# Path flags of a time-warping alignment: from VectorE comparisons to GpSimd differences and ScalarE signs

## The reference, cut to what matters

```python
def _align_one(small, large):              # for each of 32 batch elements
    D = _pairwise_euclidean(small, large)  # 256 x 256 distances
    R = _dtw_cost(D)                       # R[i,j] = D[i,j] + min(R[i-1,j], R[i,j-1], R[i-1,j-1])
    i_idx, j_idx, valid = _backtrack(R, T_small, T_large)  # from the last corner: argmin of diag, up, left
    contrib = small[i_idx] * valid[:, None].astype(small.dtype)
    return jnp.zeros((T_large, d)).at[j_idx].add(contrib)
x = x + jnp.tanh(g_xattn[1]) * vmap(_align_one)(ctx_1024, _layernorm(x, axis=-1))
```

## Time and profile before

| what | value |
|---|---|
| median of three runs | 1813.73 us |
| profiled execution, first to last instruction (span) | 1810.7 us |
| DVE busy, whole span | 1489.1 us (82%) |
| PE / ACT / POOL busy, whole span | 1379.4 / 1135.9 / 644.9 us |
| steps of the alignment, 1133.16 to 1370.00 us | DVE busy nearly throughout |
| hops L1537, x255 | 120.7 us busy, 473 ns each |
| TensorE granted clock in the alignment | 0.50 |

### The profile page before, as it was taken

One profiled execution on the slowest core, in us unless ns is written; L12 is line 12 of the kernel. 1 busy time (PEld: TensorE's weight loads), 2 busy tenths in 40 slices (PEclk: granted clock), 3 DMA queues, 4 the chain that ended last, 5 costly groups with the idle time before them and its releaser, 6 DMA issues. The chain is left out here.

```text
span 1810.7 us, 37501 instructions
## 1 busy us (share of the span) xinstructions
PE 1379.4 (76%) x11461; PEld 1067.0 (59%) x11461; DVE 1489.1 (82%) x4194; ACT 1135.9 (63%) x2463; POOL 644.9 (36%) x1094
## 2 busy tenths in 40 slices
PE   4899999999999999999999984233332004899996
PEld 4577878888888888888888764000001003666664
DVE  7777877878878787788877753999998998999995
ACT  4567677776777767777677662243334002999997
POOL 3333343433434334343343322200000003787785
PEclk7999999999999999999999996555555556999999
DMA  6444544445444454444544311322220002223321
GB/s 173 137 128 115 149 123 118 137 122 154 123 117 139 120 154 123 118 141 122 152 125 120 99 36 28 96 60 61 60 42 8 0 0 84 74 89 98 96 77 48
DMA packets 322942, 179.56 MB, mean 99 GB/s; under 512 B 93793, under 2 KB 318193, under 8 KB 322802
## 3 DMA queue, kind: packets, MB, share of 16 engines
q1 hardware_dynamic: 322802, 178.07, 35.2%
HBM read 122.91 MB, written 50.33 MB: 96 GB/s over the span
## 5 line engine op out<-in xcount | busy, mean ns | idle before, releaser
L1031 DVE TENSOR_REDUCE nmax<-s 128x2 f32<-128x512 f32 x512 | 327.5, 681 | 7.6 <-PE s L465 6.6
L737 ACT ACTIVATE pts<-s 128x512 f32<-128x512 f32 x512 | 282.3, 617 | 75.0 <-PE s L482 74.8
L1143 POOL TENSOR_TENSOR r<-rl 128x512 f32<-128x512 f32 x128 | 133.4, 1042 | 260.8 <-ACT rl L767 217.9
L465 PE MATMUL s<-kst,qst 96*128 96x256 bf16 x1024 | 158.7, 276 | 10.9 <-DVE nmax L1031 6.9
L482 PE MATMUL s<-qst,kst 128*128 128x256 bf16 x1024 | 160.3, 276 | 8.7 <-ACT pts L737 7.2
L1421 PE MATMUL gate<-diag,one 128*128 128x512 f16 x35 | 21.2, 607 | 171.9 <-DVE left L1512 171.9
L767 ACT ACTIVATE rl<-wb,fscl 128x256 f32<-128x256 f32 x256 | 108.0, 477 | 64.8 <-PE wb L568 64.8
L564 PE MATMUL wb<-x2l,wfcT 128*128 128x256 f32 x512 | 143.3, 302 | 0.7 <-ACT dd L789 0.7
L1000 DVE TENSOR_TENSOR r2l<-r,r2h 128x512 fp32r<-128x512 f32 x128 | 88.6, 692 | 66.0 <-POOL r L1143 40.3
L496 PE MATMUL oacc<-pts,vw 128*32 128x256 f32 x2048 | 137.9, 387 | 5.3 <-ACT pts L737 5.2
L431 PE MATMUL wb<-wprT,r2l 128*128 128x256 f32 x512 | 130.5, 293 | 6.9 <-DVE r2l L1000 6.9
(11 more groups left out here) (304 smaller groups left out, 4630.9 us busy)
## 6 DMA issues: line engine op xcount, KB each, us to landing
kst<-k_parts_dram SPq DMA_DIRECT2D x384, 64.0 KB, 2.6
qst<-q_parts_dram SPq DMA_DIRECT2D x384, 64.0 KB, 2.4
k_parts_dram<-kp SPq DMA_DIRECT2D x32, 384.0 KB, 5.4
q_parts_dram<-qp SPq DMA_DIRECT2D x32, 384.0 KB, 3.1
xin<-in_x_dram SPq DMA_DIRECT2D x32, 256.0 KB, 2.8
cT_raw<-in_ctx_T_dram SPq DMA_DIRECT2D x32, 256.0 KB, 5.4
xres<-in_x_dram SPq DMA_DIRECT2D x32, 256.0 KB, 3.1
cin<-in_ctx_dram SPq DMA_DIRECT2D x32, 256.0 KB, 4.7
```

Source lines behind the costliest of these rows:

```text
L465: last = pe.matmul(s1[h % 2][:, t, :], qst[b.p][0:MAXROW, h, t * P:t * P + P], kst[b.p][0:MAXROW, h, :], start=True, stop=True)
L737: act.activation(pt[h % (2 * HPG)], s2[h % 2][:], ACT.Exp).then_inc(e["expd"], 1)
L1031: v.tensor_reduce(nmax[:, T * h:T * h + T], s1[h % 2][:], AX.X, ALU.max, negate=True)\
L1143: pool.tensor_tensor(r2[:], rl[:, k % 2], rl[:, k % 2], ALU.mult)\
```

## The change

VectorE no longer makes `diag` and `left`. GpSimd subtracts instead, after every half step of 4 rows (`compare`): up minus diagonal, and left minus `best`, both into `between` (128 x 2 x 4 x 64, float32). ScalarE turns them into signs in float16 (`sign`), and TensorE weighs the signs with 0.5 and -512 into `gate`, whose row now has a 65th element, column 0. Column 0 gets the carry from the neighbour block by two small matrix products (`shift16`, `edge16`), so `top`, `carry_on` and the tile `carry` go. The decision scan runs in two halves of 4x65 elements, each 10 rows behind the first row of its half (`BEHIND`), and `far` has three buffers. The exchange of R between blocks is also made in halves; it waits until GpSimd has read what it overwrites (`compared`), and `best` of a half waits for the same. GpSimd's tables for the last layer are spread over steps 3 to 8, and its splitting of `b1` comes after the last `compare`.

```diff
+HROWS = ROWS // 2
+BEHIND = ROWS + 2
...
+            def compare(s, h):
+
+                u, p = 2 * s + h, s % 2
+                pool.wait_ge(chained, u + 1)
+                if s >= 1:
+                    pool.wait_ge(exchanged, u - 1), pool.wait_ge(flags, u - 1)
+                up_diag, row_left = apart[h][:, 0], apart[h][:, 1]
+                if h == 0:
+                    before = cost[1 - p][:, ROWS - 1, :]
+                    pool.tensor_tensor(up_diag[:, 0, :], before[:, 1:BW + 1], before[:, 0:BW], ALU.subtract)
+                lo, hi = HROWS * h + (h == 0), HROWS * h + HROWS
+                above = cost[p][:, lo - 1:hi - 1, :]
+                pool.tensor_tensor(up_diag[:, lo - HROWS * h:, :], above[:, :, 1:BW + 1], above[:, :, 0:BW], ALU.subtract)
+                pool.tensor_tensor(row_left, cost[p][:, some(h), 0:BW], best[:, some(h), :], ALU.subtract)\
+                    .then_inc(compared, 1)
...
+            for s in range(NSTEP):
+                for h in range(2):
+                    compare(s, h)
+                last_layer_tables(s - 3)
             pool.wait_ge(b1_in, 16)
...
+            def exchange(s, h):
+
+                act.wait_ge(chained, 2 * s + h + 1), act.wait_ge(compared, 2 * s + h)
                 for k in range(NBLK - 1):
...
-            def carry_on(s):
...
+            def sign(s, h):
+
+                u = 2 * s + h
+                act.wait_ge(compared, u + 1)
+                if s >= 1:
+                    act.wait_ge(gated, u - 1)
+                act.activation(signs[h][:], apart[h][:], ACT.Sign, bias=smallest[:, 0:1]).then_inc(flags, 1)
...
+                if 1 <= s < NSTEP:
+                    exchange(s - 1, 1)
+                if 1 <= s <= NSTEP:
+                    sign(s - 1, 1)
                 if s + 1 < NSTEP:
                     root(s + 1)
                 if s >= 2:
                     evacuate(s - 2)
                 if s < NSTEP - 1:
-                    exchange(s)
-                if 1 <= s < NSTEP:
-                    carry_on(s - 1)
+                    exchange(s, 0)
+                if s < NSTEP:
+                    sign(s, 0)
...
+            def gates_of(s, h):
+                u, q = 2 * s + h, s % 3
+                if s >= 1:
+                    pe.wait_ge(lasted, u - 1)
+                if s >= 1:
+                    pe.matmul(gate[h][:, :, 0], shift16[:], far[q - 1][:, some(h), BW], start=True, stop=False)
+                pe.matmul(gate[h][:, :, 0], edge16[:], unit[:, some(h)], start=(s == 0), stop=True)
+                pe.wait_ge(flags, u + 1)
+                pe.matmul(gate[h][:, :, 1:BW + 1], half16[:], signs[h][:, 0], start=True, stop=False)
+                pe.matmul(gate[h][:, :, 1:BW + 1], left16[:], signs[h][:, 1], start=False, stop=True).then_inc(gated, 1)
...
+            def behind(r):
+
+                u, at = (r - BEHIND) // HROWS, (r - BEHIND) % HROWS
+                if u >= 0 and at == 0:
+                    last_up(u // 2, u % 2)
...
                     prev = cost[p][:, i - 1, :] if i else cost[1 - p][:, ROWS - 1, :]
+                    if first and s >= 1:
+                        v.wait_ge(compared, u - 1)
                     ch.tick(v.tensor_tensor(best[:, i, :], prev[:, 1:BW + 1], prev[:, 0:BW], ALU.min))
-                    v.tensor_tensor(diag[p][:, i, :], prev[:, 0:BW], prev[:, 1:BW + 1], ALU.is_le)
-                    if i == 0 and s >= 1:
-                        v.wait_ge(exchanged, s)
+                    if first and s >= 1:
+                        v.wait_ge(exchanged, u - 1)
                     ch.hold()
...
-                    if i:
-                        v.tensor_tensor(left[p][:, i - 1, :], best[:, i - 1, :], cost[p][:, i - 1, 0:BW], ALU.is_gt)
-                    if i == ROWS // 2 and s >= 1:
-                        top(s - 1)
...
+                    behind(r)
```

More of the change, by code:

```diff
@@ L54 @@
 LEFT = 1024.0
+HROWS = ROWS // 2
+BEHIND = ROWS + 2
+CENTRE = LEFT / 2 + 0.5
+SMALLEST = 2.0 ** -126
 class Batch:
@@ L1224, in alignment_phase @@
         best = sb("best", [P, ROWS, BW])
[L1225 to L1228, removed]
+        apart = [sb(f"between{u}", [P, 2, HROWS, BW]) for u in range(2)]
+        signs = [sb(f"signs{u}", [P, 2, HROWS, BW], F16) for u in range(2)]
+        far = [sb(f"far{p}", [P, ROWS, BW + 1], F16) for p in range(3)]
         step = [sb(f"step{p}", [P, ROWS, BW], F16) for p in range(2)]
-        adds = sb("adds", [P, ROWS, BW])
-        one16, neg16, left16 = o["one16"], sb("neg16", [P, P], F16), sb("left16", [P, P], F16)
+        adds, smallest = sb("adds", [P, HROWS, BW + 1]), sb("smallest", [P, 1])
+        unit = sb("unit", [P, ROWS], F16)
+        one16, neg16, half16, left16 = o["one16"], sb("neg16", [P, P], F16), sb("half16", [P, P], F16), sb("left16", [P, P], F16)
+        shift16, edge16 = sb("shift16", [P, P], F16), sb("edge16", [P, P], F16)
         steps = sb("steps", [NB, S, S], F16)
@@ L1234, in alignment_phase @@
         hop, path = sb("hop", [NB, S]), sb("path", [NB, S + 1])
-        gate = [ctx.enter_context(nc.psum_tensor(f"gate{p}", [P, ROWS, BW], F32)) for p in range(2)]
+        gate = [ctx.enter_context(nc.psum_tensor(f"gate{h}", [P, HROWS, BW + 1], F32)) for h in range(2)]
         diff = [ctx.enter_context(nc.psum_tensor(f"diff{p}", [P, ROWS, BW], F32)) for p in range(2)]
@@ L1251, in alignment_phase @@
         g_in = [sem(f"g_in{p}") for p in range(2)]
-        (consts, zeroed, rooted, chained, flags, exchanged, gated, topped, lasted, carried, diffed, stepped, rch, held,
+        (consts, zeroed, rooted, chained, compared, flags, exchanged, gated, lasted, carried, diffed, stepped, rch, held,
          turned, copied, pch) = (sem(n) for n in (
-            "consts2", "zeroed", "rooted", "chained", "flags", "exchanged", "gated", "topped", "lasted", "carried",
+            "consts2", "zeroed", "rooted", "chained", "compared", "flags", "exchanged", "gated", "lasted", "carried",
             "diffed", "stepped", "row_chain", "held", "turned2", "path_cp", "pool_chain2"))
@@ L1262, in quad, with some @@
             return slice(NB * k, NB * k + NB)
+        def some(h):
+            return slice(HROWS * h, HROWS * h + HROWS)
         def loaded(s):
@@ L1308, in _ @@
             pc = Chain(pool, pch)
-            for p in range(2):
-                pc.link(pool.memset(carry[p][:], -2.0))
+            pc.link(pool.memset(smallest[:], SMALLEST))
+            for tile, value, base in ((half16, 0.5, 0), (left16, -LEFT / 2, 0), (one16, 1.0, 0), (neg16, -1.0, 0),
+                                      (shift16, 1.0, NB)):
+                pc.link(pool.memset(tile[:], 0.0))
+                pc.link(pool.affine_select(out=tile[:], in_=tile[:], compare_op=ALU.not_equal, fill=value,
+                                           base=base, pattern=[[-1, P]], channel_multiplier=1))
@@ L1311, in _ @@
+            pc.link(pool.memset(edge16[:], 0.0))
+            pc.link(pool.affine_select(out=edge16[0:NB, :], in_=edge16[0:NB, :], compare_op=ALU.not_equal,
+                                       fill=-CENTRE - 2.0, base=0, pattern=[[-1, P]], channel_multiplier=1))
+            pc.link(pool.memset(unit[:], 1.0))
             pc.link(pool.memset(adds[:], 2.0))
             pc.link(pool.memset(adds[:, :, 0:1], 2 * LEFT))
[L1313 to L1316, removed]
@@ L1325, in _ @@
[L1325 to L1331, removed]
@@ new lines, in last_layer_tables @@
+            def last_layer_tables(k):
+                if k == 0:
+                    pc.link(pool.memset(ones[:], 1.0))
+                    pc.link(pool.memset(o["identb"][:], 0.0))
+                    pc.link(pool.affine_select(out=o["identb"][:], in_=o["identb"][:], compare_op=ALU.not_equal, fill=1.0,
+                                               base=0, pattern=[[-1, P]], channel_multiplier=1))
+                elif k == 1:
+                    pc.link(pool.iota(o["iota"][:], pattern=[[1, S]], base=0, channel_multiplier=0,
+                                      allow_small_or_imprecise_dtypes=True))
+                    pool.sem_inc(l_consts, 1)
+                elif k == 2:
+                    pc.link(pool.memset(o["w1T"][:, C, :], 0.0))
+                elif k == 3:
+                    pc.link(pool.memset(shift[:, 0:1], MAGIC + 1.0))
+                    pc.link(pool.memset(shift[:, 1:2], 2.0))
+                elif k == 4:
+                    pc.link(pool.iota(iota[:], pattern=[[1, S]], base=0, channel_multiplier=0,
+                                      allow_small_or_imprecise_dtypes=True))
+                elif k == 5:
+                    pc.link(pool.memset(ident[:], 0.0))
+                    pc.link(pool.affine_select(out=ident[:], in_=ident[:], compare_op=ALU.not_equal, fill=1.0,
+                                               base=0, pattern=[[-1, NB]], channel_multiplier=1))
+                    pool.sem_inc(consts, 1)
@@ L1351, in root @@
```

(52 more changed lines are left out.)

25 lines of the change are left out of this document (8 added, 17 removed).

## The result

The changed kernel takes 1832.83 us (median of four runs, 1831.24 to 1834.11) against 1812.99 us (four runs) for the kernel before: 1.0106 times as long, 95% interval 1.0087 to 1.0125. It is 19.8 us slower; 29 were forecast, a median of 1843 us in a range of 1802 to 1880. The profiled execution spans 1829.5 us, 18.8 more than before.

A forecast was written before the change was run, and what follows sets the result against it. VectorE was taken to set the time. A new step of 5.04 + 1.04 + 1.5 = 7.6 us, 34 times, less 231.2 plus 2.0, gave +29 us: 1843 us, range 1802 to 1880 for 8 in 10.

The forecast's parts named there:

- The row is a dependent chain, and the comparisons lie in its gaps: VectorE's rows: without `diag` and `left` a row takes 0.63 us, eight 5.04 instead of 5.28.
- The half scans cost 0.52 each: Decision scan on VectorE: 260 elements take 0.64 us, less 0.12 idle anyway; 0.52 each, 1.04 a step.
- GpSimd's reads block `best` and the row scans, once each: VectorE's two-SBUF-input instructions wait while GpSimd reads SBUF: 1.5 us a step lost, 0.40 per 256-element read.
- the 192 elements: GpSimd's 192-element read for a step's first half: forecast to cost VectorE 0.30 us.
- the read of 64: GpSimd's 64-element read for a step's first half: forecast to cost VectorE nothing.
- The relay is hidden: GpSimd, ScalarE and TensorE between a half's last row and its decision scan: costed at nothing, 1 to 3 us to spare.
- the rival of a late relay: Half scan or `best` waits for the relay: at 0.5 us a half, step 8.6 us, time 1877 us; chance 0.12.
- The small terms: Outside the steps: step 0 +0.5 us, tail +0.5, bias parts reaching into the hops +1.0; together 2.0.
- The slots set the row: VectorE's rows: row 0.52 us, port loss 0.9, step 6.1, time 1792 us; rival, chance 0.16.
- The port costs little: GpSimd reads as quickly as its squares, 0.9 us a step; step 6.74, 1814 us, no change; rival, chance 0.10.

The follow-up runs named there:

- the experiment that does not read: Changed kernel with GpSimd's subtractions replaced by fills with 1.0, which write SBUF and read nothing: 1792.58 us, ratio 0.989.

## Why the prediction was right, and what it mis-sized

- *The row is a dependent chain, and the comparisons lie in its gaps.* Right: 0.65 in the five kernels without them, 0.63 forecast. The semaphores of the first row of a half, with two waits, add 0.07 each; the forecast left them out.
- *The half scans cost 0.52 each.* They cost 0.46: 0.58 from start to next start (1202.82 to 1203.40), not 0.64. The element price of 0.0019, drawn through the row scan's 0.26, was too low and the base too high: between the two decision scans, 1.13 for 512 and 0.58 for 260, an element costs 0.0022. Rows, half scans and waits together make 6.19 a step in the experiment that does not read, against 6.08 forecast.
- *GpSimd's reads block `best` and the row scans, once each.* Right in kind: the long ones stand where GpSimd reads, they go when it only writes, and the half scan is free. Mis-sized: 1.5 us a step forecast, 1.1 measured (7.28 less 6.19). This is the step of the sum that failed. It took 0.40 for a read of 256 elements, on the ground that GpSimd gets in when VectorE's read ends and holds VectorE for 0.51 us from there, less 0.12. In the trace GpSimd's instruction is already 0.2 us old when VectorE's next request comes (1201.11 and 1201.33; 1204.68 and 1204.90): its recorded start lies inside the VectorE instruction before. VectorE is let go 0.54 us after GpSimd's start (0.58 by the earlier trace rows), and so loses a little over 0.3. The first read of the second half cost only 0.17. The first half's scan lost 0.31, as much as was put down for the 192 elements; but it starts 0.01 us before that read, while the read of 64, put at nothing, is still running (1200.36 to 1200.69), and no run parts the two. 34 steps of 0.4 are 14 us; the rows, half scans and waits, forecast too short, took 4 of them back, and 1843 became 1833. That the two misses have opposite signs is luck.
- *The relay is hidden.* Right: one wait of 2.1 us, in the tail; so the rival of a late relay fell too. ScalarE's work came to 3.9 us a step (131.52 in 34), 3.8 forecast; before it was 2.5 (82.40 in 33 steps), not 3.1, which changes nothing in the sum.
- *The small terms.* Step 0 took 5.7 instead of 5.3 us, the tail 7.56 instead of 7.40, the hops 0.7 more: 1.3 together against 2.0.
- *The other rivals.* "The slots set the row" fell with the kernel before without comparisons, and with the bare rows of 0.65. "The port costs little" had the loss to the reads nearer than the forecast had it: 0.9 a step against 1.1 measured and 1.5 forecast. It fell on its reason and on the row: 256 elements took GpSimd 0.65 to 0.68 us and not 0.52, and a row 0.65 and not 0.60.

## What to carry to other kernels

On an engine that runs one dependent chain, count the gaps before moving work off it: what fits in them costs next to nothing where it stands (two comparisons 0.01 us a row here), unless a longer instruction could have used the gap (0.12). Work given to GpSimd was not free for VectorE here where both read SBUF and VectorE's instruction had two inputs there. It was free where VectorE took an input from PSUM or where GpSimd only wrote, and nearly free where GpSimd's reads were short copies; whether a subtraction cut into shorter ones would do as well was not run. Look in the trace for a stretch where two engines already meet: step 1 of the kernel before held the answer, and moving its reads was a gain by itself.

## What was not expected of the hardware

The cost of a GpSimd read to a dependent chain is not in proportion to its length: reads of 0.39 to 0.45 us cost at most 0.02, one of 0.68 us cost 0.32, and one of 0.34 that began just before VectorE's request cost 0.07. And the loss does not even out: the pattern of one long scan and one long `best` in each half repeats from step to step (0.66 and 0.54 us again at 1207.92 and 1208.62), as the last row of each half releases GpSimd anew.
